# A gated cross-attention block: 32x32 transposes on VectorE and a DRAM round trip for the queries' input, in place of TensorE transposes

## What is computed

```python
x = x + tanh(g_xattn) * attention(layernorm(x), ctx, Wq, Wk, Wv, Wo)   # softmax over 154 context rows
x = x + tanh(g_ffn) * ffn(layernorm(x))
# ffn(z): z_prev = z shifted by one token
#   r = sigmoid((mu_r*z + (1-mu_r)*z_prev) @ W_r.T);  k = relu((mu_k*z + (1-mu_k)*z_prev) @ W_k.T)**2
#   out = r * (k @ W_v.T)
```

## Time and profile before

| | |
|---|---|
| median of 3 runs | 1393.03 us (1392.62 to 1393.97) |
| profiled execution, its own time | 1394.31 us |
| its span, first to last instruction | 1392.6 us |
| granted TensorE clock, mean | 0.994 of full |
| busy, share of the span | PE 97%, DVE 75%, ACT 56%, POOL 43% |
| DMA packets, bytes | 99179, 84.07 MB |

### The profile page before, as it was taken

The page is one execution under the profiler, slowest core; times in us unless marked ns, Lnnn a source line. Parts: engine busy times, 40 slices in busy tenths (PEclk is TensorE's granted clock), DMA queues, the critical chain, the costliest instruction groups (busy, mean ns, idle before and its releaser), DMA issues.

```text
span 1392.6 us, 28127 instructions
## 1 busy us (share of the span) xinstructions
PE 1353.0 (97%) x9484; PEld 993.8 (71%) x9484; DVE 1038.6 (75%) x1938; ACT 779.7 (56%) x1457; POOL 596.5 (43%) x797
## 2 busy tenths in 40 slices
PE   5999999999999999999999999999999999999998
PEld 4766676777767677677777767677776777767677
DVE  6767778686776868778686876868777786877764
ACT  6654736457374655737466374655637465473633
POOL 5523435253443534435253443525345353443434
PEclk9899999999999999999999999999999999999999
DMA  9421111212021121101212111121102212111011
GB/s 299 140 76 46 40 37 60 67 53 67 19 72 45 53 75 53 50 25 64 64 53 75 34 49 45 60 67 53 58 22 66 57 53 75 53 43 32 31 47 39
DMA packets 99179, 84.07 MB, mean 60 GB/s; under 512 B 49488, under 2 KB 64336, under 8 KB 99152
## 3 DMA queue, kind: packets, MB, share of 16 engines
q1 hardware_dynamic: 99152, 83.72, 19.8%
HBM read 57.75 MB, written 20.71 MB: 56 GB/s over the span
## 4 chain that ended last, share of the span: by engine, by line
PE 81%; ACT 7%; DVE 7%; issue 2%; DMA 1%; SPq 1%; ACTq 0%; DVEq 0%
PE g_bank L1264 46%; PE g_bank L1424 7%; PE o_bank L1371 7%; PE s_bank L1345 4%; PE d_bank L1377 4%; ACT s_bank L712 3%; PE s_bank L1321 3%; ACT pq L711 3%; PE s_bank L1355 2%; PE d_bank L1270 2%; DVE buf L905 2%; PE o_bank L1270 1%; DVE o_bank L1049 1%; DVE d_bank L1049 1%; PE s_bank L1270 1%
## 5 line engine op out<-in xcount | busy, mean ns | idle before, releaser
L982 DVE TENSOR_TENSOR pq<-s_bank,pq 128x512 f16<-128x512 f32 x320 | 220.2, 689 | 70.0 <-ACT s_bank L712 69.5
L978 DVE TENSOR_REDUCE mm<-s_bank 128x3 f32<-128x462 f32 (+1 forms) x384 | 198.7, 577 | 94.2 <-PE s_bank L1321 94.2
L711 ACT ACTIVATE pq<-s_bank 128x512 f16<-128x512 f32 x320 | 192.3, 601 | 93.1 <-PE s_bank L1349 92.9
L1264 PE MATMUL g_bank<-xnT,WqT 128*128 128x512 f32 x756 | 198.4, 409 | 0.0
L712 ACT ACTIVATE s_bank<-s_bank 128x512 f32<-128x512 f32 x320 | 194.7, 608 | 0.0
L1424 PE MATMUL g_bank<-buf,WkT 128*128 128x512 f32 x720 | 188.7, 408 | 5.6 <-DVE buf L905 4.2
L1264 PE MATMUL g_bank<-WoT,buf 128*128 128x512 f32 x768 | 193.5, 401 | 0.0
L1264 PE MATMUL g_bank<-WrT,buf 128*128 128x512 f32 x744 | 184.1, 396 | 0.0
L511 POOL TENSOR_TENSOR buf<-place,buf 128x512 fp32r<-128x512 f32 x64 | 82.7, 1293 | 235.0 <-ACT buf L617 235.0
L1264 PE MATMUL g_bank<-WvT,buf 128*128 128x512 f32 x708 | 174.5, 395 | 0.0
L1264 PEld LDWEIGHTS g_bank<-WrT,buf 128*128 128x128 f32 x744 | 137.3, 188 | 39.5 <-issue 10.8
(11 more groups left out here) (166 smaller groups left out, 2122.8 us busy)
## 6 DMA issues: line engine op xcount, KB each, us to landing
xa<-in_x SPq DMA_DIRECT2D x64, 256.0 KB, 3.5
x<-in_x SPq DMA_DIRECT2D x64, 256.0 KB, 2.8
out<-x SPq DMA_DIRECT2D x48, 256.0 KB, 2.0
place<-x SPq DMA_DIRECT2D x16, 256.0 KB, 2.4
out<-place SPq DMA_DIRECT2D x16, 256.0 KB, 2.0
k_all<-k_scratch SPq DMA_DIRECT2D x15, 256.0 KB, 2.9
k_low<-k_scratch SPq DMA_DIRECT2D x15, 256.0 KB, 3.0
v_main<-v_scratch SPq DMA_DIRECT2D x15, 256.0 KB, 2.8
```

The lines of the kernel that those rows point to most:

```text
L711: nc.scalar.activation(pq[:, n, HI, :], bank[:, :], ACT.Exp, scale=SCALE).then_inc(p_hi, 1)
L978: nc.vector.reduce_max(maxima, scores, AX.X).then_inc(reduced, 1)
L982: nc.vector.tensor_tensor(pq[:, n, LO, :], score_bank[5 * g + n][:, :], pq[:, n, HI, :], ALU.subtract).then_inc(p_lo, 1)
L1264: ins = nc.tensor.matmul(dst, stationary(s, c), moving(m, c), start=(c, n) == (0, 0), stop=(c, n) == (chunks - 1, len(PRODUCTS) - 1))
```

## The change

For the blocks from 2 on (14 of 16) PE no longer transposes the queries' input. Blocks 0 and 1 are as before. In steps 1 to 14:

- SP loads block i+1 in four strips of 32 partitions (`load_strips`) so that the tokens lie in another order, 4x32 tokens of every tile's rows.
- ACT writes the normalized tile into `xn1`, two tiles of `place`, not back into `xa` (`norm1_turn`); DVE turns each 128x512 tile in squares of 32x32 (`turn`) back into `xa`.
- SP stores a half (two tiles, 512 KB) to DRAM (`store_turned`), waits for it, and loads it in four DMAs of 32 partitions, 512 pieces of 256 bytes each, into `xnT_loaded`, the memory of the low part of `xnT` (`load_turned`). This is done for h = 0 and h = 1.
- ACT makes the high parts in four pieces (`xT_high_half`), ahead of `tanh_r(i-1, 3)`; POOL makes three of the low pieces (`xT_low_half`), DVE one (`xT_low_part`).
- `query_first` makes the first query product in the order HI*HI, LO*HI, HI*LO, and waits for the low parts ahead of the last four matmuls.
- DVE's `gated(i-1, 1)` moves from inside g = 2 to its end. `load_keys(i+1)` moves behind `load_turned(i, 1)`, and `load_x1(i, 1)` and `(i, 0)` behind `load_keys`.

```diff
             def load_xa(i, t):
                 sp.dma_start(xa[:, t, :], x_tiles[i, t]).then_inc(xa_loaded[t], 16)
+            def load_strips(i):
+                for a in range(4):
+                    rows = slice(DH * a, DH * a + DH)
+                    sp.dma_start(xa[rows, :, :], x_strips[i, a]).then_inc(xa_loaded[a], 16)
+            def store_turned(i, h):
+                sp.wait_ge(xT_turned, i * TT - 2 + 2 * h)
+                sp.dma_start(xt_scratch[h], xa[:, 2 * h:2 * h + 2, :]...).then_inc(xT_stored, 16)
+            def load_turned(i, h):
+                sp.wait_ge(xT_stored, i * 32 - 16 + 16 * h)
+                squares = xt_scratch[h].rearrange("(a r) (c b) n -> b r c a n", a=4, b=4)
+                for b in range(4):
+                    rows = slice(DH * b, DH * b + DH)
+                    sp.dma_start(xnT_loaded_part[rows, :, :, h, :], squares[b]).then_inc(xT_loaded[h], 16)
...
+            def xT_low_half(i, h, part):            # POOL
+                chunks, n = slice(2 * part, 2 * part + 2), i * TT + 2 * h + part + 1
+                pool.wait_ge(xT_hi, n)
+                nc.gpsimd.tensor_tensor(xnT_part[LO][:, chunks, :, h, :], xnT_loaded_part[:, chunks, :, h, :],
+                                        xnT_part[HI][:, chunks, :, h, :].bitcast(F32), ALU.subtract).then_inc(xT_lo_pool, 1)
...
+            def norm1_turn(i, t):                   # ACT
+                if t >= 2:
+                    act.wait_ge(xT_turned, (i - 2) * TT + 2)
+                act.wait_ge(norm_ready[0], i * TT + t + 1)
+                nc.scalar.activation(xn1[t % 2], xa[:, t, :], ACT.Identity, ...).then_inc(xn1_ready, 1)
+            def xT_high_half(i, h, part):
+                act.wait_ge(xT_loaded[h], (i - 1) * 64)
+                chunks = slice(2 * part, 2 * part + 2)
+                high(xnT_part[HI][:, chunks, :, h, :], xnT_loaded_part[:, chunks, :, h, :], xT_hi)
...
                     exps(i, g, 4)
+                    if ffn and pre:
+                        for t in ((0, 1), (2, 3), ())[g - 1]:
+                            norm1_turn(i + 1, t)
+                        if g == 3:
+                            for h in range(2):
+                                for part in range(2):
+                                    xT_high_half(i + 1, h, part)
                     if ffn:
                         tanh_r(i - 1, g)
...
+            def turn(i, t):                         # DVE
+                h = t // 2
+                dve.wait_ge(xn1_ready, i * TT + 2 * h + 2)
+                nc.vector.transpose(turned[h][:, :, t % 2, :], xn1[t % 2].rearrange("p (k s) -> p k s", s=TAIL)).then_inc(xT_turned, 1)
...
                     p_low(i, g, 0)
                     p_low(i, g, 1)
-                    if ffn and g == 2:
-                        gated(i - 1, 1, V_BANK[1])
+                    if ffn and pre and g == 2:
+                        turn(i + 1, 0)
+                        turn(i + 1, 1)
...
                     p_low(i, g, 4)
-                    if ffn and g != 2:
+                    if ffn:
                         gated(i - 1, g - 1, V_BANK[g - 1])
+                    if ffn and pre and g == 2:
+                        turn(i + 1, 2)
+                        turn(i + 1, 3)
...
                     if ffn:                         # PE
                         pe.wait_ge(th_ready, i * TT)
+                        pe.wait_ge(xT_hi, (i + 2) * TT)
+                        query_first(lambda: (pe.wait_ge(xT_lo, i + 2 * TT), pe.wait_ge(xT_lo_pool, 3 * i)))
                         pe.wait_ge(u_ready, i * TT)
```

More of the change, by code:

```diff
@@ L158, in flamingo_block @@
         xT_done, xT_hi, xT_lo = sem("xT_done"), sem("xT_hi"), sem("xT_lo")
+        xT_turned, xT_stored = sem("xT_turned"), sem("xT_stored")
+        xT_lo_pool = sem("xT_lo_pool")
+        xT_loaded = [sem(f"xT_loaded{h}") for h in range(2)]
         q_done, q_hi, q_copied, q_lo = sem("q_done"), sem("q_hi"), sem("q_copied"), sem("q_lo")
@@ L379, in step @@
                 if pre:
-                    sp.wait_ge(xT_done, (i + 1) * TT)
                     sp.wait_ge(q_lo, (i + 1) * G)
[L382 to L385, removed]
+                if pre and ffn:
+                    load_strips(i + 1)
+                elif pre:
+                    for t in range(TT):
+                        load_xa(i + 1, t)
                 if ffn:
@@ L405, in step @@
                         sp.wait_ge(later_stored[n], LATER_STORES[n])
-                if pre:
+                if pre and not ffn:
                     load_keys(i + 1)
@@ L558, in step @@
                     attn_low(i, g - 1)
+                    if ffn and pre and g == 3:
+                        for h, part in ((0, 0), (0, 1), (1, 1)):
+                            xT_low_half(i + 1, h, part)
                     if ffn:
@@ L803, in step @@
                         kv_high(KV_UNITS - 1)
-                    if pre and g == 3:
+                    if pre and not ffn and g == 3:
                         xT_high(i + 1, 0)
@@ L941, in moments, with moments1 @@
                 nc.vector.bn_aggr(mv[:, which, t, :], stats[:, which, t, :]).then_inc(mean_ready[which], 1)
-            def moments1(i, t):
-                dve.wait_ge(xa_loaded[t], 16 * (i + 1))
+            def moments1(i, t, strips=False):
+                if not strips:
+                    dve.wait_ge(xa_loaded[t], 16 * (i + 1))
+                elif t == 0:
+                    for a in range(4):
+                        dve.wait_ge(xa_loaded[a], 16 * (i + 1))
                 moments(0, i, t, xa[:, t, :])
@@ L1330, in query, with query_first @@
                         before).then_inc(q_done, 1)
+            def query_first(wait_lower):
+                for n, (s, m) in enumerate(((HI, HI), (LO, HI), (HI, LO))):
+                    if m == LO:
+                        wait_lower()
+                    for c in range(C):
+                        ins = nc.tensor.matmul(Q_BANK[0][:, :], WqT[:, s, c, cols(0)], xnT[:, m, c, :], start=(n, c) == (0, 0),
+                                               stop=(n, c) == (len(PRODUCTS) - 1, C - 1))
+                ins.then_inc(q_done, 1)
             def maxima_transposed(i):
@@ L1456, in _ @@
                     pe.wait_ge(kv_lo, t + 1)
-                xT(0, t, False)
+                xT(0, t)
             pe.wait_ge(w_lo, 2 * C)
             pe.wait_ge(xT_hi, TT)
[L1461 to L1467, removed]
+            query_first(lambda: pe.wait_ge(xT_lo, TT))
             query(0, 1, False, at(1, lambda: maxima(0, 0)))
@@ L1493, in step @@
                     keys_or_values(FIRST_LATER + 1)
-                values(i, 0, pre)
+                values(i, 0, not ffn)
                 head_scores(i, 1)
@@ L1505, in step @@
                     keys_or_values(FIRST_LATER + 3)
-                values(i, 1, pre)
+                values(i, 1, not ffn)
                 head_scores(i, 2)
@@ L1517, in step @@
                     keys_or_values(FIRST_LATER + 5)
-                values(i, 2, pre)
+                values(i, 2, not ffn)
                 head_scores(i, 3)
@@ L1529, in step @@
                     ffn_v(i - 1, 2)
-                if pre:
+                else:
                     for t in range(1, TT):
-                        xT(i + 1, t, True)
-                values(i, 3, pre)
+                        xT(1, t)
+                values(i, 3, not ffn)
                 if not ffn:
```

91 lines of the change are left out of this document (56 added, 35 removed).

## The result

The changed kernel took 1403.26 us (median of 18 runs, 1396.89 to 1411.08) beside 1393.99 us of the kernel before (18 runs, 1391.76 to 1395.63): the ratio is 1.0069 [1.0059, 1.0079], slower by 0.7%. It lies inside the range (1370 to 1425), but on the other side of no change from the forecast of 1386. Its profiled execution took 1403.47 us with a span of 1401.7, 9.1 us more than before.

The account below looks back on a forecast made before the run. It took PE to bound the kernel. Of 1.75 us removed per step, 1.2 go into a new wait; 0.53 x 14 = 7.4 us off 1394.31 gives 1386.9 (1385.6 against the median), forecast 1386, range 1370 to 1425.

Parts of the forecast that it names:

- The bound and the path: PE bounds the kernel; its transposes ahead of the first query product cost 1.75 us per step, 24.5 us in 14.
- The costs at nothing: DVE's turns, POOL's subtractions, the later keys and x1 loads, and SP's strips were each costed at no added time.
- The form of the new wait: PE idle some 1.2 us ahead of the first query product, released by ACT's tanh, 14 times; ACT waiting for the eighth load.
- The first hops: SP's start of the trip: store 0 lands in 2.65 us, SP resumes after 0.23, four loads issue at 0.71 each.
- the sum of the round trip: SP's stores and loads, then ACT, let the first query product start at 591.9, not 592.43: gain 0.53 us per step.
- It shares the DMA engines with the last loads: 2.65 + 0.3: Second store of the turned tiles, behind the first half's loads: issued at 582.1, landed at 585.05.
- That load lands 2.6 us later, as the 32-partition pieces of k_tail do: Eighth load, the last of the second half: issued at 587.43, landed at 590.05.
- the high bounds of the prediction: Stores at 3.7 us and landing 3.3: query product 2.0 us late per step; with the clock, 1445 us.
- Late transfer and clock: Rival, PE's wait ahead of the first query product: longer trip, clock falls costing 1.7 us; 1418, or some 1406; chance 0.38.
- the point from which it decides: The late-transfer rival, at PE's wait for the round trip, decides from about 0.3 us more per trip.
- The forecast of a small gain: Whole kernel: 0.53 us per step at the first query product, 7.4 us in 14 steps; 1376 to 1390, chance 0.37.

Follow-up runs that it names:

- e1: Changed kernel without the stores to DRAM and loads back, output not the reference's: 1369.91 us, ratio 0.9826 to the kernel before.
- e3: Changed kernel with both stores ahead of all eight loads, a semaphore per store, and the store of results behind the loads: 1370.62 us, ratio 0.9832 to the kernel before.
- e4: Changed kernel with four unused 128x512 products in PE's idle ahead of the first query product: 1396.07 us, ratio 1.0017 to the kernel before.
- e2: Changed kernel with ACT's tanh_r(i-1, 3) ahead of the second half's high parts: 1389.79 us, ratio 0.9970 to the kernel before.
- e5: Changed kernel with only the store of results moved behind the second group of loads: 1389.73 us, ratio 0.9966 to the kernel before.
- e10: e3 plus a 64 KB store and a wait for it ahead of the second half's loads: 1427.34 us, ratio 1.0234 to the kernel before.
- e7: Changed kernel plus a 64 KB store and a wait for it ahead of the second half's loads: 1446.60 us, ratio 1.0377 to the kernel before.
- e8: e7 with twelve unused products in PE's idle: 1419.72 us, ratio 1.0175 to the kernel before.

## Why the prediction was wrong

*Right.* The bound and the path: PE, and 1.75 us of transposes a step on it; e1 measured 24.0 us for all 14 steps where 24.5 were taken. The costs at nothing: a turn took 0.65 us, attend still waits for PE and not for the turns, POOL's subtractions are not waited for, and the maxima do not wait for `k_tail`. The form of the new wait: ahead of the first query product, 14 times, released by ACT's `tanh_r`, with ACT itself waiting for the eighth load. The first hops: store 0 took 2.65 us in each of the 14 steps, as taken, SP went on 0.02 us after it where 0.23 were taken, and four issues took 2.65 us where 2.84 were.

*The step that failed* is the sum of the round trip behind those issues. "It shares the DMA engines with the last loads: 2.65 + 0.3", and 0.23 to resume, gave 3.2 us for store 1; it took 3.53 to 3.98, some 3.8 in the mean, because it runs beside the four loads of the first half; 0.3 us of that is its own issue, 0.62 us behind the loads and 0.32 us in e3. "That load lands 2.6 us later, as the 32-partition pieces of k_tail do" gave the eighth load too little: 3.15 to 4.33, in the mean 3.70. The loads of `k_tail` are a quarter of its bytes, and the 256 KB loads of the keys go out ahead of them, not 0.95 us behind as here. These are 1.7 us too little (0.6 and 1.1). Hops that were shorter than taken gave back 0.8: store 1 goes out 5.4 us behind turn 1 (586.37 after 580.98 in step 7), not 6.0 (582.1 after 576.1), and the last issues are 0.14 us shorter. That leaves 0.9 us, and the value products end 0.2 us later behind turn 1 than forecast. So the idle was 1.88 us and not 1.2, and all that the transposes had given went into it. Both measured means lie above even the high bounds of the prediction, 3.7 for the store and 3.3 for the landing. It took for both the time of a transfer in an emptier queue. It also called the 3.7 us store "the one 512 KB store there is"; the trace of before has a second one (`k_scratch<-x`), which took 5.5 us.

*The rival.* What came is "Late transfer and clock", which was given 0.38, and less of it than priced: 1403 us, where it had 1406 with a fall in half of the steps. It named the point from which it decides, 0.3 us more per trip; 0.7 us came. It priced a fall of the clock at 1.7 us from the earlier trace rows; 1.6 to 1.8 were measured. It left open how many steps fall: 3 of 14 in the profiled execution. By e4 the falls are worth 7.2 us of the 9.3 us between the medians, and e2 and e5, both without a fall behind the waits, have an idle of 1.35 us and are 0.3% faster than the kernel before. The forecast of a small gain was therefore wrong by 0.7 us of waiting in a step, about 10 us, and by the clock, about 7.

*The rule beside it.* The Trainium skill, "VectorE: DVE Perf Modes", Rules for kernel authors, advises TensorE for a 128x128 transpose where its result may go to PSUM. As the change was written the run agrees, 0.7% slower. With SP's queue in another order (e3) the same work off TensorE is 1.7% faster than with the transposes, so here the measurement goes against the rule: PE is the bound, and the trip can lie beside the exponentials.

*What stays open:* whether it is the keys behind it that slow the eighth load (e5), where the 2.4 us between e4's gain and the three falls that were seen come from, and why an idle of 2.51 us, in two steps of the profiled execution, left the clock up while one of 1.99 us did not.

## What to carry to other kernels

When work moves from the bounding engine to a chain of transfers, write the chain down hop by hop and cost each hop beside what is in flight at that moment, not by the emptiest row, and with what is issued right behind it in view (likely part of the cost here, not shown); a trip 0.7 us longer than forecast turned a gain into a loss. Look at the order of the queue before the sizes: a store that was ready stood 1.0 us behind issues of 0.66 us each, and putting it ahead of them, with the store of results behind the loads, took 33 us off with the same transfers. An idle of PE of about 2 us and more costs more than its length, and what it costs on top varies from step to step.

## What the runs showed of the hardware

- The granted clock fell behind short idles. Over all experiments none of the waits ahead of the first query product with an idle up to 1.83 us brought a fall. Between 1.99 and 2.18 us four did (three in the changed kernel, 2.00 in e10) and five did not (2.08 and 2.16 in the changed kernel, 2.01 and 2.17 in e2, 2.16 in e10). Above it 26 of 28 did; the two exceptions are the idles of 2.51 us in the changed kernel. Each fall went from 2.4 to 1.2 GHz, for 3.4 us in most (6.8 us, in part over the idle, in six of e7 and one of e10), and cost 1.6 to 1.8 us. On what it hangs whether a given idle brings a fall, no run here shows. Of the start of a kernel, which is another case, the Trainium skill says that the number of matmuls at the low clock varies between runs of one kernel ("TensorE: Matmul & The Clock Gate", Part 1).
- Unused products in the gap made a kernel faster, with the wait as long as before: 7.2 us in e4 against the changed kernel, 27 us in e8 against e7.
- One and the same 512 KB store took 2.65 us by itself, in 14 of 14 steps, 3.5 to 4.0 us behind four loads of 128 KB in 256-byte pieces, and 3.0 us with these loads issued right behind it (e3). A load of 32 partitions held the queue for 0.64 us, store 0 with its 128 partitions for 0.33.
